# Fourth attention layer: row scores in eight one-bank pieces, and a ring of five banks for the turned score groups

## The chip, the cores and the metric

The kernel runs on one core of one Trainium2 chip. The metric is the device time of one execution in microseconds (us), the median of three runs. The profile is one further execution, recorded by the hardware profiler. Its own time is given beside the span of its trace.

## The reference, cut to what matters

Four transformer layers run one after the other on x (4 batches, 256 rows, 128 columns), each an attention over a context of 1601 rows and then a feed-forward block. The change is in the fourth attention, 16 heads of 8 columns:

```python
Q = _split(q @ Wq.T + bq)          # q: layer norm of x, (4, 256, 128)
K = _split(k @ Wk.T + bk)          # k, v: ctx_1024, (4, 1601, 128)
V = _split(v @ Wv.T + bv)
scores = jnp.einsum('bhqd,bhkd->bhqk', Q, K) / np.sqrt(HEAD_DIM)
scores = jnp.where(mask == 0, -1000000000.0, scores)
attn = jax.nn.softmax(scores, axis=-1)
out = jnp.einsum('bhqk,bhkd->bhqd', attn, V)
return merged(out) @ Wo.T + bo
```

There are 4 x 16 = 64 pairs of batch and head, called units here. Each has 256 x 1601 scores.

## The kernel before, in words

The stage is `quad_attention_stage` (L1221), called once, for this layer. It computes the scores of each unit twice. The first time they are **row scores**: queries on the partitions, keys along the row, only so that VectorE can find each query's largest score. The second time they are **turned scores**: keys on the partitions, queries along the row. The maxima are added to them through six more rows of the matmul's operands, so ScalarE can take the exponent directly, and the result already lies as the product with the values wants it.

The work of one step s of the loop, on each engine:

- TensorE, `score_piece(s, n)` (L1309 to L1321): row scores of unit s in four pieces (two halves of the 128-query tiles, and two halves of the keys, 801 and 800 wide). One piece fills 801 of the 1024 columns of a double bank, `S_WIDE[n % 2]`, by two matmuls (512 and 289 or 288 columns). The two double banks take turns. The piece waits until VectorE has drained the piece two before it (semaphore `drained`).
- VectorE, `maximum(s, n)` (L1480 to L1494): waits for the piece (`scored`), adds the mask and takes the maximum. In the trace it is a CUSTOM_DVE_ANT_0 and a short DVE_READ_ACCUMULATOR2_ANT behind it. After each second unit one TENSOR_REDUCE (L1494, called nmx below) joins the maxima.
- GpSimd cuts the maxima in three bf16 parts (L1467 to L1473), TensorE brings them into rows (`rows(s)`, L1346, in even steps), and ScalarE copies them to the operands `qx` (L1447).
- TensorE, `turned_group(s, g)` (L1323 to L1337): turned scores of unit s - 3 (`TURN = 3`) in seven groups W0 to W6 of two key tiles each (W6 has one). A key tile is a mask matmul (L1335) and a score matmul (L1336), 256 columns each, added up in one bank. The groups, the rows and two rarer items take banks from the ring `BANKS` in turn, three banks before. A group waits until the item that had its bank three items earlier has been read (`bank_free`, L1296).
- ScalarE, `exponent(s, g)` (L1431): the exponent of one group, bank to SBUF.
- TensorE, `values(s)` (L1364): each four units make a quad. Its product with the values stands in two chunks at the front of two successive steps, 28 and 24 matmuls in fp32. So two steps of four have such a chunk. `turn_u` (L1375) turns the result once in each quad, and VectorE's `normalise` (L1504 to L1507) divides by the sum.

All engines run their own queue in program order. TensorE's order in a step, in which S0 to S3 are the four score pieces, is written out by hand:

```python
for s in range(LAST):
    values(s)
    turned_group(s, 0)
    score_piece(s, 0)
    turned_group(s, 1)
    turned_group(s, 2)
    score_piece(s, 1)
```

and then mix, W3, rows, turn_u, W4, S2, W5, output, S3, W6. VectorE does maxima 0, 1, 2, then `normalise`, then maximum 3. SyncE loads the operands of a unit once the turned scores of the unit six before it are through (`RING = 6`). PSUM has eight banks: three in the ring, one for the values' product, and the two double banks of the row scores.

Of the kernel before, what the change touches and what calls it, by code (L numbers as in the profile page):

```python
# [7 lines left out]
F32 = mybir.dt.float32  # L8
BF16 = mybir.dt.bfloat16
I32 = mybir.dt.int32  # L10
ALU = mybir.AluOpType
# [3 lines left out]
P = 128  # L15
D = 128
B, S, SC = 4, 256, 1601
# [5 lines left out]
LOWEST = -3.0e38  # L23
# [1197 lines left out]
def quad_attention_stage(core, name, acc, wot, load_operands, load_values, ks, qx, vs, mask, maskT):  # L1221
# [3 lines left out]
    UNITS, QUADS = B * HEADS, B * HEADS // 4  # L1225
    RING, PRT, V_RING = 6, 6, 3
    TURN = 3
    half = (SC + 1) // 2
    PIECES = [(qt, at, min(half, SC - at)) for qt in range(2) for at in (0, half)]
    GROUPS = [(kt, min(2, KT - kt)) for kt in range(0, KT, 2)]  # L1230
    NG = len(GROUPS)
    CHUNKS = [(0, 7), (7, KT)]
# [3 lines left out]
     recip_done, normed, mixed, mixed_out, out_ready, added, setup) = (core.sem(f"{name}_{s}") for s in names)  # L1236
    loaded = [core.sem(f"{name}_loaded{i}") for i in range(RING)]
    v_loaded = [core.sem(f"{name}_v_loaded{i}") for i in range(V_RING)]
    S_WIDE, BANKS, U_BANK = core.wide, core.bank[0:3], core.bank[3]
    LAST = UNITS + TURN + 4  # L1240

    with ExitStack() as ctx:
        junk = core.sb(ctx, name + "_junk", [P, 2, half], F32)
        prT = core.sb(ctx, name + "_prT", [P, PRT, KT, S], F32)
        mx = core.sb(ctx, name + "_mx", [P, 2, 2, 2, 2], F32)
        nmx = core.sb(ctx, name + "_nmx", [P, 2, 2, 2], F32)
        rest = core.sb(ctx, name + "_rest", [P, 2, 2], F32)
        zero = core.sb(ctx, name + "_zero", [P, 2, 2], F32)
# [27 lines left out]
        at_slot = {slot: n for n, slot in enumerate(slots)}  # L1276

        def bank_of(s, item):
            return BANKS[at_slot[s, item] % 3]

        @block.sync
        def _(sp):
# [11 lines left out]
        @block.tensor  # L1294
        def _(pe):
            def bank_free(s, item):  # L1296
                if at_slot[s, item] < 3:
                    return
                t, before = slots[at_slot[s, item] - 3]
                if before == "rows":  # L1300
                    pe.wait_ge(rows_in, pair_rows(t) + 1)
                elif before == "mix":
                    pe.wait_ge(mixed_out, batch_end(t) + 1)
                elif before == "out":
                    pe.wait_ge(added, batch_end(t) + 1)
                else:
                    pe.wait_ge(exp_done, NG * (t - TURN) + int(before[1:]) + 1)

            def score_piece(s, n):  # L1309
                if not s < UNITS:  # L1310
                    return
                if n == 0:
                    pe.wait_ge(loaded[s % RING], 32 * (s // RING + 1))
                if 4 * s + n >= 2:
                    pe.wait_ge(drained, 4 * s + n - 1)
                qt, at, w = PIECES[n]
                for c in range(0, w, 512):
                    m = min(512, w - c)
                    ins = pe.matmul(S_WIDE[n % 2][:, c:c + m], qx[0:72, s % RING, qt * P:(qt + 1) * P],  # L1319
                                    ks[0:72, s % RING, at + c:at + c + m], start=True, stop=True)  # L1320
                ins.then_inc(scored, 1)  # L1321

            def turned_group(s, g):  # L1323
# [45 lines left out]
            def turn_u(s):  # L1369
                if quad_chunk(s) is None or quad_chunk(s)[1] != len(CHUNKS) - 1:  # L1370
                    return
                q = quad_chunk(s)[0]
                pe.wait_ge(u_out, q + 1)
                for qt in range(2):
                    ins = pe.transpose(U_BANK[:, S + qt * P:S + (qt + 1) * P], u_sb[:, qt * P:(qt + 1) * P], core.ident[:, :])  # L1375
                ins.then_inc(u_turned, 1)
# [20 lines left out]
                ins.then_inc(out_ready, 1)  # L1397

            for s in range(LAST):
                values(s)  # L1400
                turned_group(s, 0)
                score_piece(s, 0)
                turned_group(s, 1)
                turned_group(s, 2)
                score_piece(s, 1)
                mix(s)
                turned_group(s, 3)
                rows(s)
                turn_u(s)
                turned_group(s, 4)  # L1410
                score_piece(s, 2)
                turned_group(s, 5)
                output(s)
                score_piece(s, 3)
                turned_group(s, 6)

        @block.scalar
        def _(act):
# [56 lines left out]
        @block.vector  # L1475
        def _(dve):
            dve.memset(prT[:, :, KT - 1, :], 0.0).then_inc(setup, 1)
            dve.memset(U_BANK[:, 0:S], 0.0).then_inc(setup, 1)

            def maximum(s, n):  # L1480
                if not s < UNITS:
                    return
                p, e = s // 2, s % 2
                qt, at, w = PIECES[n]
                dve.wait_ge(scored, 4 * s + n + 1)
                if e == 0 and n == 0 and p >= 2:
                    dve.wait_ge(max_ready, p - 1)
                dve.tensor_tensor_reduce(junk[:, n % 2, 0:w], S_WIDE[n % 2][:, 0:w], mask(qt, at, w), 1.0, LOWEST, ALU.add, ALU.max,  # L1488
                                         mx[:, p % 2, qt, e, n % 2:n % 2 + 1]).then_inc(drained, 1)
                if e == 1 and n == 3:  # L1490
                    dve.wait_ge(drained, 4 * s + 4)
                    if p >= 2:
                        dve.wait_ge(cut_done, p - 1)
                    dve.tensor_reduce(nmx[:, p % 2, :, :], mx[:, p % 2, :, :, :], X, ALU.max, negate=True).then_inc(max_ready, 1)  # L1494

            def normalise(s):
                if quad_chunk(s) is None or quad_chunk(s)[1] != len(CHUNKS) - 1:
                    return
                q = quad_chunk(s)[0]
                lanes = U_BANK[:, S:2 * S].rearrange("p (t j c) -> p t j c", t=2, j=4)  # L1500
                dve.wait_ge(u_turned, q + 1)
                if q % 4 == 0 and q > 0:
                    dve.wait_ge(mixed, q // 4)
                dve.reciprocal(rtot[:, :, :], lanes[:, :, :, 8]).then_inc(recip_done, 1)  # L1504
                dve.wait_ge(recip_done, q + 1)
                out = heads_out[:, :, q % 4 * 32:(q % 4 + 1) * 32].rearrange("p t (j d) -> p t j d", j=4)
                dve.tensor_tensor(out, lanes[:, :, :, 0:8], rtot[:, :, :].unsqueeze(3).broadcast_to([P, 2, 4, 8]),  # L1507
                                  ALU.mult).then_inc(normed, 1)

            for s in range(LAST):  # L1510
                maximum(s, 0)
                maximum(s, 1)
                maximum(s, 2)
                normalise(s)
                maximum(s, 3)
                if batch_end(s) is not None:
                    b = batch_end(s)
                    tiles = acc[:, 2 * b:2 * b + 2, :]
                    dve.wait_ge(out_ready, b + 1)
                    dve.tensor_tensor(tiles, tiles, bank_of(s, "out")[:, 0:S].rearrange("p (t d) -> p t d", t=2),  # L1520
                                      ALU.add).then_inc(added, 1)
            dve.wait_ge(added, B)
# [602 lines left out]
def pair_layer(core, name, acc, wq, wk, wv, wo):  # L2125
# [29 lines left out]

    PIECES = [(0, 1024), (1024, SC - 1024)]

# [398 lines left out]
```

## Time and profile before

| | before |
|---|---|
| median of 3 runs | 2402.89 us (2401.49 to 2403.2) |
| profiled execution, its own time | 2405.89 us |
| span of its trace | 2404.1 us |
| mean granted TensorE clock | 0.911 |
| TensorE busy, whole span | 2066.4 us (86%) |
| VectorE busy, whole span | 1358.7 us (57%) |
| ScalarE busy, whole span | 1327.5 us (55%) |
| the stage that is changed | first row score at 1960.7 us, last at 2339.0 us |

A matmul's record is longer than the time for which it holds the engine, since matmuls overlap. What TensorE spends on one is read as the distance from its start to the start of the next. A granted clock of 1.00 is the 2.4 GHz level; a lower mean in a window is a mixture with the 1.2 GHz level. PEld is TensorE's load of the weights for the next matmul; "issue" as the releaser means that the profile shows nothing that was waited for.

### The profile page before, as it was taken

What the parts mean: (1) busy time and instruction counts of PE and PEld (TensorE: products, weight loads), DVE (VectorE), ACT (ScalarE), POOL (GpSimd) and SP (SyncE); (2) the same over time, 40 slices, a digit from 0 to 9 for tenths busy, and PEclk for the clock granted to TensorE, in tenths of its full rate; (3) what the DMA queues carried; (4) which work ended last, traced back from release to release, by engine and by line L of the source; (5) the groups of instructions that cost most, each with busy time, mean ns of one, the idle gap of its engine ahead of it and who ended that gap; (6) DMA issues with size and microseconds to landing.
All of it is one profiled execution on the core that took longest, in us unless ns stands there. A gap on an engine that the chain in (4) does not pass through costs nothing. (4 is left out here: it accounts for less than half of the span.)

```text
span 2404.1 us, 44599 instructions
## 1 busy us (share of the span) xinstructions
PE 2066.4 (86%) x17629; PEld 1438.3 (60%) x17629; DVE 1358.7 (57%) x3398; ACT 1327.5 (55%) x2088; POOL 100.6 (4%) x335
## 2 busy tenths in 40 slices
PE   5499999945844799799999999999994559999997
PEld 3377777723632467577777777777772326666663
DVE  4588888865442521555555545545545556666662
ACT  3499999931312733355555555555552326676763
POOL 1000000000011200000000000000000310000000
PEclk9699999976875989899999999999996669999997
DMA  6411111103232011000000000000000631111110
GB/s 216 168 58 53 53 56 54 46 14 114 80 102 89 4 36 35 36 1 1 1 1 1 1 1 1 2 1 1 1 1 10 228 117 60 52 59 54 58 37 13
DMA packets 50709, 115.32 MB, mean 48 GB/s; under 512 B 6476, under 2 KB 26732, under 8 KB 50508
## 3 DMA queue, kind: packets, MB, share of 16 engines
q1 hardware_dynamic: 44172, 82.25, 11.0%
q0 software_dynamic: 6336, 30.28, 3.6%
q8 instruction: 139, 2.28, 0.4%
q14 instruction: 62, 0.51, 0.1%
HBM read 81.71 MB, written 30.80 MB: 47 GB/s over the span
## 5 line engine op out<-in xcount | busy, mean ns | idle before, releaser
L2316 ACT ACTIVATE a_prT<-bank 128x512 f32<-128x512 f32 (+1 forms) x448 | 232.7, 565 | 328.0 <-PE bank L2225 327.8
L1488 DVE CUSTOM_DVE_ANT_0 a_attn_junk<-wide,a_mask 128x801 f32<-128x801 f32 (+1 forms) x256 | 247.0, 992 | 125.5 <-PE wide L1319 124.1
L1431 ACT ACTIVATE a_attn_prT<-bank 128x512 f32<-128x512 f32 (+1 forms) x448 | 237.2, 566 | 119.7 <-PE bank L1336 98.3
L2341 DVE CUSTOM_DVE_ANT_0 a_sc<-wide,a_zeros 128x1024 f32<-128x1024 f32 (+1 forms) x256 | 243.1, 988 | 91.8 <-PE wide L2211 91.8
L1777 DVE CUSTOM_DVE_ANT_0 a_attn_sc<-wide,a_mask 128x801 f32<-128x801 f32 (+1 forms) x256 | 252.9, 989 | 18.4 <-PE wide L1631 16.2
L1647 PE MATMUL bank<-ident,a_attn_sc 128*128 128x128 f32 x1664 | 244.9, 276 | 15.3 <-ACT a_attn_prT L1736 14.1
L1647 PEld LDWEIGHTS bank<-ident,a_attn_sc 128*128 128x128 f32 x1664 | 198.8, 141 | 62.6 <-issue 42.7
L2225 PE MATMUL bank<-ident,a_sc 128*128 128x128 f32 x1664 | 231.2, 277 | 1.5 <-ACT a_prT L2316 1.5
L2225 PEld LDWEIGHTS bank<-ident,a_sc 128*128 128x128 f32 x1664 | 185.4, 141 | 54.4 <-issue 28.1
L1742 ACT ACTIVATE a_attn_sc<-a_attn_sc,a_attn_nmx 128x1601 f32<-128x1601 f32 x128 | 209.6, 1638 | 8.5 <-DVE a_attn_nmx L1783 8.5
L2211 PE MATMUL wide<-a_kT,a_qT 64*128 64x512 f32 (+1 forms) x1024 | 211.0, 529 | 0.0
L2277 PEld LDWEIGHTS bank<-a_prT,a_vt 128*64 128x64 f32 x3328 | 180.3, 137 | 48.4 <-issue 47.0
L2325 ACT ACTIVATE a_sc<-a_sc,a_nmx 128x1601 f32<-128x1601 f32 x128 | 207.1, 1623 | 3.4 <-DVE a_nmx L2368 3.4
L1335 PE MATMUL bank<-a_maskT,identb 128*128 128x256 bf16 (+1 forms) x832 | 201.2, 275 | 2.2 <-DVE x L1520 1.9
L1336 PE MATMUL bank<-a_qx,a_ks 128*128 128x256 bf16 (+1 forms) x832 | 199.9, 273 | 0.0
L2277 PE MATMUL bank<-a_prT,a_vt 128*64 128x128 f32 x3328 | 195.8, 275 | 0.9 <-ACT a_prT L2316 0.9
L1736 ACT ACTIVATE a_attn_prT<-bank 128x512 f32<-128x512 f32 x320 | 172.6, 582 | 31.5 <-PE bank L1647 28.7
L1631 PE MATMUL wide<-a_ks,a_qx 72*128 72x512 bf16 (+2 forms) x512 | 152.6, 340 | 9.3 <-DMA a_qx<-a_q_stack 8.4
L2211 PEld LDWEIGHTS wide<-a_kT,a_qT 64*128 64x128 f32 x1024 | 88.6, 186 | 102.4 <-issue 93.2
L1319 PE MATMUL wide<-a_ks,a_qx 72*128 72x512 bf16 (+2 forms) x512 | 134.2, 345 | 9.6 <-DMA a_qx<-a_q_stack 8.3
L2242 PE MATMUL bank<-a_wv,ctxT 128*128 128x128 f32 x832 | 119.4, 282 | 1.3 <-ACT a_vt L2316 0.7
L2236 PE MATMUL bank<-ctxT,a_wk 128*128 128x512 f32 (+1 forms) x256 | 117.3, 543 | 2.7 <-ACT a_kT L2316 1.4
(432 smaller groups left out, 2800.7 us busy)
## 6 DMA issues: line engine op xcount, KB each, us to landing
a_ks<-a_k_parts SPq DMA_DIRECT2D x128, 225.1 KB
a_proj_ctxb<-in_ctxT SPq DMA_DIRECT2D x12, 832.0 KB, 5.1
a_k_parts<-a_proj_kp POOLq DMA_DIRECT2D x24, 416.0 KB, 5.7
a_v_rows<-a_proj_vb POOLq DMA_DIRECT2D x8, 936.0 KB, 8.4
a_vs<-a_v_rows SPq DMA_DIRECT2D x32, 234.0 KB
a_q_stack<-a_proj_qp POOLq DMA_DIRECT2D x18, 256.0 KB, 4.4
a_qx<-a_q_stack SPq DMA_DIRECT2D x128, 36.0 KB
ctxT<-in_ctxT SPq DMA_DIRECT2D x4, 832.0 KB, 12.7
```

Source lines behind the costliest of these rows:

```text
L1335: pe.matmul(out, core.identb[:, 0:keys], maskT(kt + j), start=True, stop=False)
L1431: act.activation(prT[0:keys, u % PRT, kt:kt + m, :], bank_of(s, f"W{g}")[0:keys, 0:m * S].rearrange("p (t q) -> p t q", q=S), ACT.Exp).the ...
L1488: dve.tensor_tensor_reduce(junk[:, n % 2, 0:w], S_WIDE[n % 2][:, 0:w], mask(qt, at, w), 1.0, LOWEST, ALU.add, ALU.max, mx[:, p % 2, qt, e, ...
L1647: ins = pe.transpose(bank_of(s, f"T{g}")[:, j * P:(j + 1) * P], sc[:, u % 2, qt, kt * P:(kt + 1) * P], core.ident[:, :])
L1742: act.activation(sc[:, s % 2, qt, 0:SC], sc[:, s % 2, qt, 0:SC], ACT.Exp, bias=nmx[:, s % 2, qt:qt + 1], scale=1.0).then_inc(exp_done, 1)
L1777: dve.tensor_tensor_reduce(sc[:, s % 2, qt, at:at + w], S_WIDE[n % 2][:, 0:w], mask(qt, at, w), 1.0, LOWEST, ALU.add, ALU.max, mx[:, s % 2 ...
L2211: ins = pe.matmul(S_WIDE[h][:, c:c + w], qT[rows, slot, qt * P:(qt + 1) * P], kT[rows, slot, at + c:at + c + w], start=True, stop=True)
L2225: ins = pe.transpose(RING[k % 3][:, (j % 4) * P:(j % 4 + 1) * P], flat(t)[:, j * P:(j + 1) * P], core.ident[:, :])
L2277: ins = pe.matmul(U_BANK[DH * h:DH * (h + 1), 0:P], vt[:, slot, kt, DH * h:DH * (h + 1)], prT[:, KT * h + kt, :], start=(kt == 0), stop=(k ...
L2316: copy = lambda out, src: act.activation(out, src, ACT.Copy)
L2325: act.activation(sc[:, s % 2, h, 0:SC], sc[:, s % 2, h, 0:SC], ACT.Exp, bias=nmx[:, s % 2, h:h + 1], scale=1.0, accum_out=tot[:, s % 4, h: ...
L2341: dve.tensor_tensor_reduce(sc[:, s % 2, h, at:at + w], S_WIDE[h][:, 0:w], zeros[:, 0:w], 1.0, LOWEST, ALU.add, ALU.max, mx[:, s % 2, h, p: ...
```

## The change

The row scores of a unit come in eight pieces (four of up to 401 keys for each of the two query tiles, 401, 401, 401 and 398), one matmul and one bank each. Two banks, 4 and 5 (together the former `wide0`), take turns. Banks 6 and 7 (the former `wide1`) join the ring, which has five banks then. TensorE's order is written anew, and VectorE takes eight maxima for a unit.

```diff
--- before.py
+++ after.py
@@ -1225,8 +1225,10 @@
     UNITS, QUADS = B * HEADS, B * HEADS // 4
     RING, PRT, V_RING = 6, 6, 3
     TURN = 3
-    half = (SC + 1) // 2
-    PIECES = [(qt, at, min(half, SC - at)) for qt in range(2) for at in (0, half)]
+    PARTS = 4
+    width = (SC + PARTS - 1) // PARTS
+    PIECES = [(qt, at, min(width, SC - at)) for qt in range(2) for at in range(0, SC, width)]
+    NP = len(PIECES)
     GROUPS = [(kt, min(2, KT - kt)) for kt in range(0, KT, 2)]
     NG = len(GROUPS)
     CHUNKS = [(0, 7), (7, KT)]
@@ -1236,13 +1238,14 @@
      recip_done, normed, mixed, mixed_out, out_ready, added, setup) = (core.sem(f"{name}_{s}") for s in names)
     loaded = [core.sem(f"{name}_loaded{i}") for i in range(RING)]
     v_loaded = [core.sem(f"{name}_v_loaded{i}") for i in range(V_RING)]
-    S_WIDE, BANKS, U_BANK = core.wide, core.bank[0:3], core.bank[3]
+    S_BANK, BANKS, U_BANK = core.bank[4:6], core.bank[0:3] + core.bank[6:8], core.bank[3]
+    NB = len(BANKS)
     LAST = UNITS + TURN + 4
 
     with ExitStack() as ctx:
-        junk = core.sb(ctx, name + "_junk", [P, 2, half], F32)
+        junk = core.sb(ctx, name + "_junk", [P, 2, width], F32)
         prT = core.sb(ctx, name + "_prT", [P, PRT, KT, S], F32)
-        mx = core.sb(ctx, name + "_mx", [P, 2, 2, 2, 2], F32)
+        mx = core.sb(ctx, name + "_mx", [P, 2, 2, 2, PARTS], F32)
         nmx = core.sb(ctx, name + "_nmx", [P, 2, 2, 2], F32)
         rest = core.sb(ctx, name + "_rest", [P, 2, 2], F32)
         zero = core.sb(ctx, name + "_zero", [P, 2, 2], F32)
@@ -1276,7 +1279,7 @@
         at_slot = {slot: n for n, slot in enumerate(slots)}
 
         def bank_of(s, item):
-            return BANKS[at_slot[s, item] % 3]
+            return BANKS[at_slot[s, item] % NB]
 
         @block.sync
         def _(sp):
@@ -1294,9 +1297,9 @@
         @block.tensor
         def _(pe):
             def bank_free(s, item):
-                if at_slot[s, item] < 3:
+                if at_slot[s, item] < NB:
                     return
-                t, before = slots[at_slot[s, item] - 3]
+                t, before = slots[at_slot[s, item] - NB]
                 if before == "rows":
                     pe.wait_ge(rows_in, pair_rows(t) + 1)
                 elif before == "mix":
@@ -1311,13 +1314,11 @@
                     return
                 if n == 0:
                     pe.wait_ge(loaded[s % RING], 32 * (s // RING + 1))
-                if 4 * s + n >= 2:
-                    pe.wait_ge(drained, 4 * s + n - 1)
+                if NP * s + n >= 2:
+                    pe.wait_ge(drained, NP * s + n - 1)
                 qt, at, w = PIECES[n]
-                for c in range(0, w, 512):
-                    m = min(512, w - c)
-                    ins = pe.matmul(S_WIDE[n % 2][:, c:c + m], qx[0:72, s % RING, qt * P:(qt + 1) * P],
-                                    ks[0:72, s % RING, at + c:at + c + m], start=True, stop=True)
+                ins = pe.matmul(S_BANK[n % 2][:, 0:w], qx[0:72, s % RING, qt * P:(qt + 1) * P],
+                                ks[0:72, s % RING, at:at + w], start=True, stop=True)
                 ins.then_inc(scored, 1)
 
             def turned_group(s, g):
@@ -1397,22 +1398,26 @@
                 ins.then_inc(out_ready, 1)
 
             for s in range(LAST):
+                score_piece(s, 0)
                 values(s)
                 turned_group(s, 0)
-                score_piece(s, 0)
+                score_piece(s, 1)
                 turned_group(s, 1)
+                score_piece(s, 2)
                 turned_group(s, 2)
-                score_piece(s, 1)
+                score_piece(s, 3)
                 mix(s)
                 turned_group(s, 3)
                 rows(s)
                 turn_u(s)
+                score_piece(s, 4)
                 turned_group(s, 4)
-                score_piece(s, 2)
+                score_piece(s, 5)
                 turned_group(s, 5)
                 output(s)
-                score_piece(s, 3)
+                score_piece(s, 6)
                 turned_group(s, 6)
+                score_piece(s, 7)
 
         @block.scalar
         def _(act):
@@ -1482,13 +1487,13 @@
                     return
                 p, e = s // 2, s % 2
                 qt, at, w = PIECES[n]
-                dve.wait_ge(scored, 4 * s + n + 1)
+                dve.wait_ge(scored, NP * s + n + 1)
                 if e == 0 and n == 0 and p >= 2:
                     dve.wait_ge(max_ready, p - 1)
-                dve.tensor_tensor_reduce(junk[:, n % 2, 0:w], S_WIDE[n % 2][:, 0:w], mask(qt, at, w), 1.0, LOWEST, ALU.add, ALU.max,
-                                         mx[:, p % 2, qt, e, n % 2:n % 2 + 1]).then_inc(drained, 1)
-                if e == 1 and n == 3:
-                    dve.wait_ge(drained, 4 * s + 4)
+                dve.tensor_tensor_reduce(junk[:, n % 2, 0:w], S_BANK[n % 2][:, 0:w], mask(qt, at, w), 1.0, LOWEST,
+                                         ALU.add, ALU.max, mx[:, p % 2, qt, e, n % PARTS:n % PARTS + 1]).then_inc(drained, 1)
+                if e == 1 and n == NP - 1:
+                    dve.wait_ge(drained, NP * (s + 1))
                     if p >= 2:
                         dve.wait_ge(cut_done, p - 1)
                     dve.tensor_reduce(nmx[:, p % 2, :, :], mx[:, p % 2, :, :, :], X, ALU.max, negate=True).then_inc(max_ready, 1)
@@ -1508,11 +1513,11 @@
                                   ALU.mult).then_inc(normed, 1)
 
             for s in range(LAST):
-                maximum(s, 0)
-                maximum(s, 1)
-                maximum(s, 2)
+                for n in range(6):
+                    maximum(s, n)
                 normalise(s)
-                maximum(s, 3)
+                maximum(s, 6)
+                maximum(s, 7)
                 if batch_end(s) is not None:
                     b = batch_end(s)
                     tiles = acc[:, 2 * b:2 * b + 2, :]
```

What stands in the queues of before and of the changed kernel is shown at two places.

TensorE before, from the last groups of one step to the next (L1319 is a score piece, L1335 and L1336 a turned group, L1364 the values):

```order
L1336 MATMUL bank1<-a3_qx,a3_ks 128x256
L1319 MATMUL wide1<-a3_ks,a3_qx 128x512
L1319 MATMUL wide1<-a3_ks,a3_qx 128x288
L1335 MATMUL bank2<-a3_maskT,identb 65x256
L1336 MATMUL bank2<-a3_qx,a3_ks 65x256
L1364 MATMUL bank3<-a3_attn_prT,a3_vs 9x256 x24
L1335 MATMUL bank0<-a3_maskT,identb 128x256
L1336 MATMUL bank0<-a3_qx,a3_ks 128x256
L1335 MATMUL bank0<-a3_maskT,identb 128x256
L1336 MATMUL bank0<-a3_qx,a3_ks 128x256
L1319 MATMUL wide0<-a3_ks,a3_qx 128x512
L1319 MATMUL wide0<-a3_ks,a3_qx 128x289
```

The same place on TensorE in the changed kernel (its L1320 is a score piece, L1336 and L1337 a turned group, L1365 the values):

```order
L1337 MATMUL bank0<-a3_qx,a3_ks 128x256
L1320 MATMUL wide0<-a3_ks,a3_qx 128x401
L1336 MATMUL bank1<-a3_maskT,identb 65x256
L1337 MATMUL bank1<-a3_qx,a3_ks 65x256
L1320 MATMUL wide0<-a3_ks,a3_qx 128x398
L1320 MATMUL wide0<-a3_ks,a3_qx 128x401
L1365 MATMUL bank3<-a3_attn_prT,a3_vs 9x256 x24
L1336 MATMUL bank2<-a3_maskT,identb 128x256
L1337 MATMUL bank2<-a3_qx,a3_ks 128x256
```

The last group of a step has one key tile. Before, it and the whole W0 of the next step (and the values, where there are some) stood between S3 and S0. Now S6, the short W6, S7 and the next unit's S0 follow one another, with nothing between S7 and S0, and the values come behind S0.

VectorE before, around the join of the maxima (ISA with two operands is the maximum, ISA without one reads it out):

```order
L1488 ISA a3_attn_mx 128x1
L1488 ISA a3_attn_junk,a3_attn_mx<-wide1,a3_mask 128x800
L1488 ISA a3_attn_mx 128x1
L1488 ISA a3_attn_junk,a3_attn_mx<-wide0,a3_mask 128x801
L1488 ISA a3_attn_mx 128x1
```

VectorE in the changed kernel:

```order
L1493 ISA a3_attn_junk,a3_attn_mx<-wide0,a3_mask 128x401
L1493 ISA a3_attn_mx 128x1
L1493 ISA a3_attn_junk,a3_attn_mx<-wide0,a3_mask 128x398
L1493 ISA a3_attn_mx 128x1
L1499 TENSOR_REDUCE a3_attn_nmx<-a3_attn_mx 128x4
L1493 ISA a3_attn_junk,a3_attn_mx<-wide0,a3_mask 128x401
```

Each maximum covers half the columns, and there are twice as many, all out of the two banks of the former `wide0`.

## Rows read from the trace of the kernel before

**Rows 1.** The page: span, and granted clock in 40 slices
```profile
span 2404.1 us, 44599 instructions
PEclk9699999976875989899999999999996669999997
```
**Rows 2.** Windows: length; PE, PEld, DVE, ACT, POOL busy; PEclk; DMA share; GB/s
```profile
400.00:500.00 100.00, 96.04 (x1015) 70.04 (x1017) 80.08 (x188) 88.22 (x115) 0.00 (x0) 1.00 0.12 38
600.00:640.00 40.00, 32.20 (x141) 20.71 (x141) 19.23 (x69) 13.26 (x19) 0.53 (x1) 0.79 0.34 131
...
2070.00:2110.00 40.00, 39.33 (x395) 26.93 (x394) 27.07 (x61) 27.15 (x53) 2.47 (x12) 1.00 0.16 47
```
**Rows 3.** Waits, 1950 to 2360 us: who <- whom: us in total, times, longest
```profile
DVE a_attn_junk L1488 <- PE wide L1319: 124.1, 119, 5.0
ACT a_attn_prT L1431 <- PE bank L1336: 98.3, 38, 3.3
...
PEld bank L1335 <- issue: 14.2, 34, 0.5
...
PEld bank L1346 <- POOL a_attn_parts L1473: 4.0, 14, 1.3
...
PEld bank L1335 <- ACT a_attn_prT L1431: 2.1, 11, 0.3
...
PE wide L1319 <- DVE a_attn_mx L1488: 1.2, 4, 0.4
```
**Rows 4.** Timeline of PE, a step's end: start us, us, engine, line
```profile
2119.69 0.51 PE L1319 MATMUL wide<-a_ks,a_qx 72*128 72x512 bf16 x2
2120.04 0.27 PE L1335 MATMUL bank<-a_maskT,identb 128*128 128x256 bf16 x1
...
2120.47 0.51 PE L1319 MATMUL wide<-a_ks,a_qx 72*128 72x512 bf16 x2
2120.82 0.27 PE L1335 MATMUL bank<-a_maskT,identb 128*65 128x256 bf16 x1
...
2121.13 2.56 PE L1364 MATMUL bank<-a_attn_prT,a_vs 128*9 128x256 f32 x44
```
**Rows 5.** Timeline of DVE in the same stretch
```profile
2120.24 1.00 DVE L1488 CUSTOM_DVE_ANT_0 a_attn_junk<-wide,a_mask 128x801 f32<-128x801 f32 x1 [0.22 <-PE wide L1319]
...
2121.15 0.99 DVE L1488 CUSTOM_DVE_ANT_0 a_attn_junk<-wide,a_mask 128x800 f32<-128x800 f32 x1
2122.07 0.08 DVE L1488 DVE_READ_ACCUMULATOR2_ANT a_attn_mx<- 128x1 f32 x1
2122.18 0.16 DVE L1494 TENSOR_REDUCE a_attn_nmx<-a_attn_mx 128x4 f32<-128x8 f32 x1
```
**Rows 6.** Timeline of DVE in the third layer: the same operation, 577 wide
```profile
1509.08 0.75 DVE L2341 CUSTOM_DVE_ANT_0 a_sc<-wide,a_zeros 128x577 f32<-128x577 f32 x1
...
1509.75 0.76 DVE L2341 CUSTOM_DVE_ANT_0 a_sc<-wide,a_zeros 128x577 f32<-128x577 f32 x1
```
**Rows 7.** Timeline of the stage's first steps, at a clock below full
```profile
1962.48 0.08 DVE L1488 DVE_READ_ACCUMULATOR2_ANT a_attn_mx<- 128x1 f32 x1
...
1962.62 0.13 PEld L1319 LDWEIGHTS wide<-a_ks,a_qx 72*128 72x128 bf16 x2 [1.15 <-DVE a_attn_mx L1488]
...
1966.58 0.13 PEld L1319 LDWEIGHTS wide<-a_ks,a_qx 72*128 72x128 bf16 x2 [0.97 <-DVE a_attn_mx L1488]
```
**Rows 8.** Timeline, full clock: POOL lets the rows' matmuls go
```profile
2159.14 0.21 POOL L1473 TENSOR_TENSOR a_attn_parts<-a_attn_rest,a_attn_parts 128x4 bf16<-128x4 f32 x1
...
2159.43 0.09 PEld L1346 LDWEIGHTS bank<-identb,a_attn_parts 128*6 128x6 bf16 x2 [0.21 <-POOL a_attn_parts L1473]
...
2159.63 0.28 PE L1335 MATMUL bank<-a_maskT,identb 128*128 128x256 bf16 x1
```
**Rows 9.** Timeline of DVE: normalise in two successive quads
```profile
2128.85 0.20 DVE L1504 RECIPROCAL a_attn_rtot<-bank 128x8 f32<-128x8 f32 x1
...
2129.23 0.98 DVE L1488 CUSTOM_DVE_ANT_0 a_attn_junk<-wide,a_mask 128x800 f32<-128x800 f32 x1
...
2152.78 0.20 DVE L1504 RECIPROCAL a_attn_rtot<-bank 128x8 f32<-128x8 f32 x1
```

## The prediction, on record before the changed kernel ran

> **What bounds the kernel now.** I read the windows first, then the waits, then the timeline. The changed stage runs at the end of the program, and the slices of the page show the clock near full there [rows 1]. In a window of the stage TensorE is busy for 39.33 of 40 us at a granted clock of 1.00, the 2.4 GHz level, while VectorE and ScalarE are busy for 27 us each [rows 2]. The waits say the same: VectorE waits 124.1 us for score pieces and ScalarE 98.3 us for turned groups, while TensorE's matmuls waited 1.2 us for VectorE, in 4 cases at the stage's start; a weight load waited 2.1 us for ScalarE, in 11 cases [rows 3]. So TensorE's queue is the path. Every 0.1 us that it stands still in each of the 64 steps costs 6.4 us, and VectorE has only to keep out of its way.
>
> The timeline gives TensorE's prices. A piece of 801 columns holds it from 2119.69 to 2120.04, 0.35 us. From there to the next piece are one whole group, 0.43 us. The short W6 stands from 2120.82 to about 2121.03 (two matmuls at 0.108), 0.22 us, and then the values start [rows 4]. A quad takes 2152.78 - 2128.85 = 23.93 us [rows 9].
>
> **What the change takes and adds on TensorE.** The columns stay the same (1601 for each query tile), and so does the number of score matmuls, 8 per unit: 512 + 289 becomes 401 + 401. By the row, 401 columns take 0.35 x 401/801 = 0.17 us [rows 4]. Groups, values and loads are the same. The streaming term is 0. The operands of S0 are wanted earlier by the length of the values, at most 3 us; SyncE orders them steps ahead, at the end of the turned group of the unit six before, so I put it at nothing.
>
> **The ring of five banks.** It can only remove waits for a bank. They are the 2.1 us above [rows 3], 0.1% of the time. ScalarE's 98.3 us of waiting is not cured by banks, since TensorE produces groups no faster. I take -2 us, with 0 as the other end.
>
> **The two banks of the row scores: the round.** A bank is used in a round: matmul, VectorE's maximum, release, next matmul. Its parts:
> - From the start of a piece to the start of its maximum: 2119.69 to 2120.24 is 0.55 us for 801 columns [rows 4, 5]. 0.34 of it is streaming, so the latency is 0.21 and for 401 columns it makes 0.17 + 0.21 = 0.38 us.
> - From a maximum to the next thing that VectorE can start: 0.91 us at 801 columns [rows 5] and 0.67 at 577 [rows 6]. That is 0.00107 us a column, so 401 columns take 0.67 - 176 x 0.00107 = 0.48 us. If none of it shrank below the 577 row it would be 0.67, the upper bound. I take 0.49.
> - From there (the start of the read-out) to TensorE's weight load: 1962.48 to 1962.62, 0.14 us [rows 7]. A load that has waited isn't hidden behind a running matmul. At the rows' matmuls GpSimd ends at 2159.35, the load starts at 2159.43, and the next group starts at 2159.63; the two small matmuls stream for 0.11 us, so streaming began near 2159.52, 0.09 after the load began [rows 8]. That gives 0.24 us together, 0.14 at least.
>
> The round is 0.38 + 0.49 + 0.24 = 1.11 us, and 1.01 with the lower end. So piece n + 2 can't start earlier than 1.11 us behind piece n.
>
> **Where TensorE gives that much time and where not.** With a whole group between pieces it comes to the piece after next 2 x (0.17 + 0.43) = 1.20 us later. That is more than 1.11, so there is no wait. At the end of a step it is different: S6 0.17, W6 0.22, S7 0.17, and then S0 of the next unit at once, 0.56 us behind S6. S0 needs the bank of S6. The wait is 1.11 - 0.56 = 0.55 us (0.45 with the lower end), in every step, also where the values follow, since they stand behind S0. S7 itself waits 0.13 us for the bank of S5, which is inside the same sum. Before, the pieces were 1.2, 1.2 and more, 0.78 and 1.2 us apart and the same comparison never failed. All of W0, the values and the groups are queued behind S0, and ScalarE waits for them.
>
> I work it out for the 60 boundaries that have turned groups and a next unit (steps 3 to 62): 60 x 0.55 = 33.0 us. Once in a quad `normalise` stands between maxima 5 and 6. It delays the next maximum by the 0.38 us from the reciprocal to the next maximum [rows 9]. VectorE was free 0.11 us before S6's maximum was due, so S0 is late by another 0.27 us: 14 x 0.27 = 3.8 us. The join nmx starts 0.11 us after a read-out begins and delays the maximum of S0 [rows 5]; that adds about 0.05 us for S2 in one step of four, 0.7 us in all.
>
> **The start.** In steps 0 to 2 there are no groups. Before, such a step took 1966.58 - 1962.62 = 3.96 us [rows 7]. At half the clock a round is 0.33 + 0.21 + 0.49 + 0.24 = 1.27 us, eight pieces 5.1 us, so 3 x 1.1 = +3.3 us.
>
> **Given back.** The rows' matmuls waited 4.0 us for GpSimd in 14 cases [rows 3]. The maxima of a pair are complete at about the same place as before, and `rows` stands later behind it by the new wait, so some of this goes: -1 us.
>
> **Sum.** +33.0 + 3.8 + 0.7 + 3.3 - 2 - 1 = +37.8 us on the profiled execution's 2405.89, which lies 3.0 us above the median of the runs. Against the median: 2402.89 + 38 = 2441 us, 1.6% slower. The lower ends (0.45 a boundary, nothing for the start, 5 us given back) leave 27.0 + 4.5 - 5 = +26, so 2429.
>
> **A rule that speaks against it.** In the window of the stage the clock was granted in full with TensorE busy for 98% [rows 2]. With the new waits a quad takes 23.93 + 2.5 = 26.4 us and TensorE is busy for 90% of it. The nearest rows on both sides are 96% busy at 1.00 and 80% busy at 0.79 [rows 2]. The Trainium skill, page "TensorE: Matmul & The Clock Gate", section "A second HAM failure mode: psum-queue depth-cycling", says that short pauses between groups of matmuls that cycle through PSUM banks can make the clock swing between its two levels. No row here shows that for pauses of half a microsecond, so it is only a rival.
>
> **The rivals.**
> 1. *The round is longer than 1.20 us.* Then a wait arises at every second piece as well. If the maximum of 401 columns cost 0.67 us, as at 577, the round would be 1.29 us: 0.73 us at each boundary and 0.09 at each of three more pairs, 1.0 us a step, so 60 + 4 + 6 = +70 us, 2473. For it: a cost that doesn't halve with the width is unseen below 577. Against it: the two widths give a straight line through nearly nothing but columns. Chance 0.13.
> 2. *The clock falls.* If TensorE ran at 1.2 GHz for a tenth of the stage's 380 us, that tenth would do half its work, another 38 us: 2479. Against it: pauses are short and the stage stays 90% busy. Chance 0.06.
> 3. *No change.* The wait at S0 is made good elsewhere, because TensorE wasn't the path after all. Then its busy 39.33 of 40 us would have to hide idle time, such as the 14.2 us at 34 loads put down to issue [rows 3]. Time within 5 us of 2403. Chance 0.05.
> 4. *Faster.* The five banks count for more: if these 14.2 us before the groups are waits for a bank, and the round hides behind a ring in which groups run ahead, the sum is -14.2 - 2.1 = -16 us, 2387. It decides if the load waits at L1335 vanish and S0 shows none. Against it: the loads wait where the piece ahead still streams, and the matmuls behind show no gap. And the round at S0 is a sum of durations that I read, of which 0.38 + 0.49 alone exceeds the 0.56 available. Chance 0.04.
>
> **How the numbers follow.** My forecast (waits at the step boundary only, 2425 to 2450) has a chance of 0.72. A measurement of this kernel tells about 0.2%, 5 us, from no change. Slower: 0.72 + 0.13 + 0.06 = 0.91, same 0.05, faster 0.04. The predicted time is that of the forecast, 2441. The range has to leave out no more than 2 in 10: below it reaches 2420, since the faster cases hold 0.09, and above 2468, which takes in most of rival 1.
>
> **What the profile after would show.** If I am right: L1320 waits for the maximum (L1493) once in each step, about 0.5 us, at S0; VectorE's maximum lasts about 0.57 us with a pitch of 0.49; the quad takes 26 to 27 us; the clock stays at 1.00; no wait of L1336 for ScalarE. A wait at pieces with a whole group between them means rival 1. A clock under 1.00 in the middle of the stage means rival 2. A quad of 24 us or less means that my reading of the path is wrong.

## The result, and the profile after

| | before | changed |
|---|---|---|
| median on the same chip | 2402.45 us (4 runs, 2401.49 to 2403.2) | 2437.77 us (4 runs, 2436.13 to 2440.51) |
| ratio, 95% interval | | 1.0148 [1.0131, 1.0166] |
| span of the profiled execution | 2404.1 us | 2434.4 us |

The change made the kernel 35 us slower; 38 us were forecast. First, from the page of the changed kernel, the granted clock in 40 slices, VectorE's maximum and the score matmul:

```profile
PEclk9799999966966899999999999999995679999997
...
L1493 DVE CUSTOM_DVE_ANT_0 a_attn_junk<-wide,a_mask 128x401 f32<-128x401 f32 (+1 forms) x512 | 287.2, 574 | 122.5 <-PE wide L1320 113.9
...
L1320 PE MATMUL wide<-a_ks,a_qx 72*128 72x401 bf16 (+1 forms) x512 | 176.6, 346 | 36.2 <-DVE a_attn_mx L1493 27.7
```

The score matmuls (now L1320) have idle time ahead of them, and it ends with VectorE's maximum. The waits of the stage show the same pair, 27.7 us in 71 cases, where it was 1.2 us in 4 [rows 3]:

```profile
ACT a_attn_prT L1436 <- PE bank L1337: 94.8, 42, 4.0
ACT a_attn_prT L1436 <- PE wide L1337: 54.9, 27, 4.0
PEld wide L1320 <- issue: 40.6, 63, 0.8
...
PE wide L1320 <- DVE a_attn_mx L1493: 27.7, 71, 0.6
...
PEld bank L1336 <- issue: 8.2, 19, 0.4
...
PEld wide L1336 <- issue: 4.7, 11, 0.4
...
PEld bank L1347 <- POOL a_attn_parts L1478: 0.3, 1, 0.3
```

The 63 loads put down to issue (40.6 us) are those of the 63 pieces S0 behind the first: the load stands behind the same wait as its matmul, and the profile names no releaser for it. No line has a wait of the turned groups for ScalarE any more, and ScalarE waits longer than before, 150 us. The timeline of TensorE shows the end of a step without values. It answers to [rows 4]:

```profile
2119.79 0.34 PE L1320 MATMUL wide<-a_ks,a_qx 72*128 72x401 bf16 x1
...
2120.40 0.34 PE L1320 MATMUL wide<-a_ks,a_qx 72*128 72x401 bf16 x1
2120.58 0.27 PE L1336 MATMUL wide<-a_maskT,identb 128*65 128x256 bf16 x1
2120.69 0.27 PE L1337 MATMUL wide<-a_qx,a_ks 128*65 128x256 bf16 x1
2120.80 0.34 PE L1320 MATMUL wide<-a_ks,a_qx 72*128 72x398 bf16 x1
2121.50 0.33 PE L1320 MATMUL wide<-a_ks,a_qx 72*128 72x401 bf16 x1 [0.36 <-DVE a_attn_mx L1493]
```

```profile
2121.47 0.10 PEld L1320 LDWEIGHTS wide<-a_ks,a_qx 72*128 72x128 bf16 x1 [0.58 <-issue]
```

S5 starts at 2119.79, S6 at 2120.40, S7 at 2120.80 and S0 at 2121.50, that is 1.10 us behind S6. S7 streams for 0.17 us, so TensorE stands for 0.53 us. The 0.36 in the record is less, because the record of S7 runs on after its columns are in. VectorE at the same moment, to be read with [rows 5]:

```profile
2120.66 0.08 DVE L1493 DVE_READ_ACCUMULATOR2_ANT a_attn_mx<- 128x1 f32 x1
2120.77 0.58 DVE L1493 CUSTOM_DVE_ANT_0 a_attn_junk<-wide,a_mask 128x401 f32<-128x401 f32 x1
2121.27 0.08 DVE L1493 DVE_READ_ACCUMULATOR2_ANT a_attn_mx<- 128x1 f32 x1
2121.27 0.57 DVE L1493 CUSTOM_DVE_ANT_0 a_attn_junk<-wide,a_mask 128x398 f32<-128x398 f32 x1
```

S6 starts, 0.37 us later its maximum, 0.50 us later the read-out, 0.23 us later S0. That is the whole round of the bank that S0 takes. The steady steps repeat it: S0 stands for 0.53 us in 46 of the 60 boundaries that the prediction counted and for 0.79 us in the other 14, those with `normalise` ahead, 35.4 us in all. In the step with `normalise` it is longer, and a quad, read from one reciprocal to the next, has gone from 23.93 us [rows 9] to 26.47 us (of `normalise`, the reciprocal is its first instruction):

```profile
2115.64 0.20 DVE L1509 RECIPROCAL a_attn_rtot<-bank 128x8 f32<-128x8 f32 x1
...
2142.11 0.20 DVE L1509 RECIPROCAL a_attn_rtot<-bank 128x8 f32<-128x8 f32 x1
```

```profile
2141.84 0.34 PE L1320 MATMUL wide<-a_ks,a_qx 72*128 72x401 bf16 x1
...
2142.25 0.34 PE L1320 MATMUL wide<-a_ks,a_qx 72*128 72x398 bf16 x1
2143.21 0.33 PE L1320 MATMUL wide<-a_ks,a_qx 72*128 72x401 bf16 x1 [0.62 <-DVE a_attn_mx L1493]
```

Here S0 comes 1.37 us behind S6 and TensorE stands for 0.79 us. The window that answers to [rows 2] shows TensorE busy for 37.39 of 40 us, with the clock still at 1.00:

```profile
2070.00:2110.00 40.00, 37.39 (x394) 23.69 (x396) 26.93 (x98) 23.34 (x45) 2.47 (x12) 1.00 0.18 53
```

The start of the stage answers to [rows 7]:

```profile
1956.46 0.85 PE L1320 MATMUL wide<-a_ks,a_qx 72*128 72x401 bf16 x2 [8.27 <-DMA a_qx<-a_q_stack]
...
1961.33 0.92 PE L1320 MATMUL wide<-a_ks,a_qx 72*128 72x401 bf16 x2 [0.28 <-DVE a_attn_mx L1493]
...
2387.15 5.80 PE L1365 MATMUL bank<-a_attn_prT,a_vs 128*9 128x256 f32 x104 [0.47 <-ACT a_attn_prT L1436]
```

Eight pieces take 4.87 us there, where four took 3.96, both at the clock's lower level (0.50). From the first score piece (1956.46) to the start of the last product with the values (2387.15) the stage takes 430.7 us. Before, the same two points lay 392.4 us apart (1960.68 and 2353.09), so the stage is 38.3 us longer. The spans differ by 30.3 us only: in this pair of profiles the code ahead of the stage took 4.2 us less and the code behind it 3.8 us less, though neither was touched. Single executions of one kernel lie that far apart (29 runs of the kernel before on one chip: 2393 to 2405 us).

### The profile page after: what moved, and what is told of

It is laid out like the page before. It is cut to its first block and busy times, and to the rows that moved or that the text cites. A ratio compares the mean times of both kernels' runs of the same rounds, so it can differ in the third digit from the quotient of the medians.

```text
span 2434.4 us, 45111 instructions
## 1 busy us (share of the span) xinstructions
PE 2071.1 (85%) x17629; PEld 1435.8 (59%) x17629; DVE 1400.7 (58%) x3910; ACT 1329.4 (55%) x2088; POOL 100.6 (4%) x335
## 5 line engine op out<-in xcount | busy, mean ns | idle before, releaser
L1493 DVE CUSTOM_DVE_ANT_0 a_attn_junk<-wide,a_mask 128x401 f32<-128x401 f32 (+1 forms) x512 | 287.2, 574 | 122.5 <-PE wide L1320 113.9
L1320 PE MATMUL wide<-a_ks,a_qx 72*128 72x401 bf16 (+1 forms) x512 | 176.6, 346 | 36.2 <-DVE a_attn_mx L1493 27.7
L1436 ACT ACTIVATE a_attn_prT<-bank 128x512 f32<-128x512 f32 (+1 forms) x271 | 146.8, 565 | 96.9 <-PE bank L1337 94.8
L1636 PE MATMUL wide<-a_ks,a_qx 72*128 72x512 bf16 (+2 forms) x512 | 152.4, 340 | 9.3 <-DMA a_qx<-a_q_stack 8.5
L1436 ACT ACTIVATE a_attn_prT<-wide 128x512 f32<-128x512 f32 (+1 forms) x177 | 97.1, 569 | 56.2 <-PE wide L1337 54.9
L1336 PE MATMUL bank<-a_maskT,identb 128*128 128x256 bf16 (+1 forms) x501 | 124.9, 274 | 0.0
L1337 PE MATMUL bank<-a_qx,a_ks 128*128 128x256 bf16 (+1 forms) x501 | 124.0, 273 | 0.0
```

What stands on the lines that cost most here:

```text
L1320: ins = pe.matmul(S_BANK[n % 2][:, 0:w], qx[0:72, s % RING, qt * P:(qt + 1) * P], ks[0:72, s % RING, at:at + w], start=True, stop=True)
L1436: act.activation(prT[0:keys, u % PRT, kt:kt + m, :], bank_of(s, f"W{g}")[0:keys, 0:m * S].rearrange("p (t q) -> p t q", q=S), ACT.Exp).the ...
L1493: dve.tensor_tensor_reduce(junk[:, n % 2, 0:w], S_BANK[n % 2][:, 0:w], mask(qt, at, w), 1.0, LOWEST, ALU.add, ALU.max, mx[:, p % 2, qt, e, ...
```

## The experiments

The theory: two banks are one too few. A bank comes round in 1.10 us, and at the end of a step TensorE wants it after 0.56. The rivals were: the number of pieces costs (semaphore waits, more instructions); the order costs (S0 ahead of the values); the ring of five gives something back and hides a larger loss. Each ratio below is against the kernel before on the same chip, with its 95% interval.

**Three banks for the row scores, four in the ring.** Pieces and order stay.

```diff
-    S_BANK, BANKS, U_BANK = core.bank[4:6], core.bank[0:3] + core.bank[6:8], core.bank[3]
+    S_BANK, BANKS, U_BANK = core.bank[4:7], core.bank[0:3] + core.bank[7:8], core.bank[3]
+    NS = len(S_BANK)
...
-                if NP * s + n >= 2:
-                    pe.wait_ge(drained, NP * s + n - 1)
+                if NP * s + n >= NS:
+                    pe.wait_ge(drained, NP * s + n - NS + 1)
```

(The bank and the scratch tile of a piece are then numbered by `(NP * s + n) % NS`.)

> Eight pieces and the changed order stay, the row scores get three banks (4, 5, 6) and the ring four. Theory of the round: a bank is wanted again by the third piece behind it. At the boundary of a step that is S5 to S0, 0.17 + 0.43 + 0.17 + 0.22 + 0.17 = 1.16 us, more than the round of 1.10, so the wait at S0 vanishes in every step, a quad takes about 23.9 us again, and in steps 0 to 2 VectorE's pitch of 0.50 us rules (eight pieces 4.0 us). Time 2402 us, between 2397 and 2407. Rival, the number of pieces costs (twice the semaphore waits and instructions on TensorE and VectorE): the time stays near 2437 us whatever the banks. Rival, the order costs (S0 ahead of the values): it stays near 2437 us too.

Measured: 2400.02 us against 2399.67, ratio 1.0 [0.999, 1.0011]. One bank more takes the loss away as far as the times can tell (0.1%, under 3 us), with eight pieces and with S0 ahead of the values. So neither of the rivals on pieces and order can be what cost 35 us. TensorE's timeline at the end of a step:

```profile
2106.57 0.34 PE L1321 MATMUL wide<-a_ks,a_qx 72*128 72x401 bf16 x1
2106.96 0.51 PE L1321 MATMUL wide<-a_ks,a_qx 72*128 72x398 bf16 x2
2107.40 3.21 PE L1366 MATMUL bank<-a_attn_prT,a_vs 128*9 128x256 f32 x56
```

S7 and S0 are one record of two now (x2), 0.51 us long: S0 starts at 2106.96 + 0.51 - 0.34 = 2107.13, right behind S7's 0.17 us of columns. The wait of 0.53 us is gone. A little is left all the same: a quad takes 24.18 us, where about 23.9 were expected, and the stage takes 394.0 us (1952.92 to 2346.91), 1.6 more than before. The runs with `turn_u` later, below, show where it lies.

```profile
2097.95 0.20 DVE L1510 RECIPROCAL a_attn_rtot<-bank 128x8 f32<-128x8 f32 x1
...
2122.13 0.20 DVE L1510 RECIPROCAL a_attn_rtot<-bank 128x8 f32<-128x8 f32 x1
```

**Four banks, a ring of three.** As above with `core.bank[4:8]` and `core.bank[0:3]`.

> As the run with three banks, but four banks for the row scores (4 to 7) and the ring of three as before the change. Theory of the round: no wait at S0; a ring of three costs what it cost before, 2 to 3 us in all; time 2403 us, between 2398 and 2408. Rival, a longer ring is worth something of its own: this run is slower than the one with four banks in the ring by 5 us or more.

Measured: 2399.63 us against 2399.67, ratio 1.0004 [0.9993, 1.0015]. On balance nothing changes: the stage takes 394.0 us again. The traces show two small effects that cancel. With the fourth bank a steady quad takes 24.07 us instead of 24.18; with the shorter ring each of the three quads over the end of a batch takes 25.43 us instead of 24.99.

**Two banks, a ring of three.** The changed kernel with banks 6 and 7 unused.

```diff
-    S_BANK, BANKS, U_BANK = core.bank[4:6], core.bank[0:3] + core.bank[6:8], core.bank[3]
+    S_BANK, BANKS, U_BANK = core.bank[4:6], core.bank[0:3], core.bank[3]
```

> The changed kernel with banks 6 and 7 left unused: two banks for the row scores, a ring of three. Theory: the ring of five is worth nothing to 2 us, since TensorE is the path and hardly waits for a bank; time 2438 us, between 2435 and 2443, quad 26.5 us. Rival, the five banks did give something back and hid a larger loss: this run is slower than the changed kernel by 5 to 16 us.

Measured: 2441.19 us against 2399.67, ratio 1.0174 [1.0158, 1.019]. The interval overlaps that of the changed kernel, [1.0131, 1.0166], which comes from another set of runs, so the times alone don't rule out the rival's smaller values (1.0174 against 1.0148 is 6 us). The profile decides. Its waits have the same line as the changed kernel's, and a quad is as long:

```profile
PE wide L1320 <- DVE a_attn_mx L1493: 27.7, 71, 0.6
...
PEld bank L1336 <- ACT a_attn_prT L1436: 1.8, 10, 0.3
```

```profile
2116.38 0.20 DVE L1509 RECIPROCAL a_attn_rtot<-bank 128x8 f32<-128x8 f32 x1
...
2142.84 0.20 DVE L1509 RECIPROCAL a_attn_rtot<-bank 128x8 f32<-128x8 f32 x1
```

26.46 us. From the first score (1958.02) to the last product (2388.65) the stage takes 430.6 us, against 430.7 with the ring of five. The two banks that the ring gained in the change are worth nothing there.

**Another order with two banks.** Ring of five as in the change.

```diff
-                score_piece(s, 0)
                 values(s)
                 turned_group(s, 0)
-                score_piece(s, 1)
+                score_piece(s, 0)
                 turned_group(s, 1)
-                score_piece(s, 2)
+                score_piece(s, 1)
                 turned_group(s, 2)
-                score_piece(s, 3)
+                score_piece(s, 2)
                 mix(s)
                 turned_group(s, 3)
+                score_piece(s, 3)
                 rows(s)
```

> Two banks and a ring of five as in the changed kernel, only TensorE's order is another: values, W0, S0, W1, S1, W2, S2, W3, S3, rows, turn_u, S4, then as changed. S7 and S0 have W0 between them, and the pair without a group between is S3, S4. Theory of the round (1.10 us): in steps without rows the wait moves to S4, 1.11 - 0.77 = 0.34 us, and S7 waits 0.12; in steps with rows 0.04 and 0.12; about 1.2 us a quad, and 0.3 for normalise, against 2.5 in the changed kernel. So about 15 us less than the changed kernel: 2421 us, between 2414 and 2428. Rival, the cost lies in the pieces and not in their places: 2437 us.

Measured: 2413.63 us against 2399.67, ratio 1.0058 [1.0039, 1.0077]. By the ratios that is 21 us less than the changed kernel, by place alone; 15 were expected, and the time lies just under the expected range. Why more, the timeline shows at a step with values and without rows:

```profile
2100.77 0.34 PE L1320 MATMUL wide<-a_ks,a_qx 72*128 72x401 bf16 x1
2101.38 0.75 PE L1320 MATMUL wide<-a_ks,a_qx 72*128 72x398 bf16 x2
```

```profile
2101.64 0.08 DVE L1493 DVE_READ_ACCUMULATOR2_ANT a_attn_mx<- 128x1 f32 x1
```

S3 and S4 are one record, so S4 starts at 2101.38 + 0.75 - 0.34 = 2101.79, only 1.02 us behind S2 and 0.15 us after the read-out of S2's maximum. The round was 1.11 in my sum and is 1.02 here. TensorE stands for 0.24 us (S3's columns were in at 2101.55), so S4 cost 0.24 us in such a step instead of 0.34, and S7 nothing instead of 0.12. S0 stands for 0.34 us once in a quad, in the step with `normalise`, and for 0.08 us in one step more:

```profile
2116.39 0.08 DVE L1493 DVE_READ_ACCUMULATOR2_ANT a_attn_mx<- 128x1 f32 x1
```

```profile
2116.43 0.27 PE L1337 MATMUL bank<-a_qx,a_ks 128*128 128x256 bf16 x1
2116.62 0.33 PE L1320 MATMUL wide<-a_ks,a_qx 72*128 72x401 bf16 x1
```

The group ahead of this S0 is in at 2116.43 + 0.11 = 2116.54, and S0 starts 0.23 us after the read-out of S6's maximum, not 0.15; the last section comes back to this. A quad takes 24.87 us, 0.9 more than before; 1.5 were expected.

**Half of the maximum.** The changed kernel; each maximum reads 200 of 401 columns and leaves out the rest. TensorE has the same work, pieces and waits.

```diff
-                dve.tensor_tensor_reduce(junk[:, n % 2, 0:w], S_BANK[n % 2][:, 0:w], mask(qt, at, w), 1.0, LOWEST,
+                h = w // 2
+                dve.tensor_tensor_reduce(junk[:, n % 2, 0:h], S_BANK[n % 2][:, 0:h], mask(qt, at, h), 1.0, LOWEST,
```

> The changed kernel, but each of VectorE's maxima reads only the first half of its piece's columns (200 of 401; the other half is left out of the maximum). TensorE's work, its order, the number of pieces and all waits stay. Theory of the round: the maximum's pitch falls from 0.50 to about 0.29 us, the round from 1.10 to 0.89, the wait at S0 from 0.53 to 0.32 us in every step and from 0.79 to about 0.37 in the step with normalise, 1.1 us a quad, and the start gets 2 us shorter. Time about 18 us less than the changed kernel, that is 17 us above before (between 12 and 23). Rival, twice as many pieces and semaphore waits cost as such: no difference to the changed kernel, 35 us above before.

Measured: 2419.43 us against 2401.69, ratio 1.0079 [1.0057, 1.0102], 18 us above before (17 expected). TensorE's wait for the maximum, and one place of it:

```profile
PE wide L1320 <- DVE a_attn_mx L1494: 11.4, 63, 0.2
```

```profile
2113.97 0.08 DVE L1494 DVE_READ_ACCUMULATOR2_ANT a_attn_mx<- 128x1 f32 x1
```

```profile
2113.70 0.33 PE L1320 MATMUL wide<-a_ks,a_qx 72*128 72x398 bf16 x1
2114.21 0.33 PE L1320 MATMUL wide<-a_ks,a_qx 72*128 72x401 bf16 x1 [0.17 <-DVE a_attn_mx L1494]
```

S0 comes 0.34 us after S7's columns, where it was 0.53; the forecast was 0.32. VectorE was idle for about a third of the window before and after the change (27.07 and 26.93 of 40 us busy), and it sets TensorE's time through the length of a single instruction.

**Three banks, and turn_u later.**

```diff
                 rows(s)
-                turn_u(s)
                 score_piece(s, 4)
                 turned_group(s, 4)
+                turn_u(s)
```

> Three banks for the row scores and four in the ring, and turn_u behind W4 instead of behind the rows, so that ScalarE's copy of the values' product has 0.6 us more. In the run with three banks turn_u starts 0.43 us behind the rows' matmuls, which stream for 0.11. Theory: about 0.2 us a quad, 3 us in all, come back against that run: 1 to 4 us under before, so within what can hardly be told. Rival: the later normalise delays maxima 5 to 7 and S0 waits instead, no gain.

Measured: 2397.93 us against 2401.69, ratio 0.9986 [0.9974, 0.9998]. A quad takes 23.92 us, 0.26 less than with three banks alone, so what that run had left over lies at `turn_u`:

```profile
2097.20 0.20 DVE L1510 RECIPROCAL a_attn_rtot<-bank 128x8 f32<-128x8 f32 x1
...
2121.12 0.20 DVE L1510 RECIPROCAL a_attn_rtot<-bank 128x8 f32<-128x8 f32 x1
```

**Three banks, turn_u later, spread order.** The edits of the three-bank, the other-order and the last run together, with turn_u behind W4.

> As the run before, and TensorE's order is the spread one (values, W0, S0, W1, S1, W2, S2, W3, S3, rows, S4, W4, turn_u, S5, W5, S6, W6, S7). No bank is wanted sooner than 1.37 us. Theory: no wait for VectorE is left, also not in the step with normalise (0.1 us a quad in the run with three banks), a quad takes 23.7 to 23.8 us. 2 to 5 us under before. Rival: TensorE has no more to give and the time is that of before.

Measured: 2396.17 us against 2401.69, ratio 0.9987 [0.9973, 1.0]. A quad takes 23.80 us:

```profile
2097.33 0.20 DVE L1510 RECIPROCAL a_attn_rtot<-bank 128x8 f32<-128x8 f32 x1
...
2121.13 0.20 DVE L1510 RECIPROCAL a_attn_rtot<-bank 128x8 f32<-128x8 f32 x1
```

**The kernel before with turn_u later.** Four pieces in two double banks.

```diff
                 rows(s)
-                turn_u(s)
                 turned_group(s, 4)
+                turn_u(s)
```

> The kernel before with four pieces in two double banks, only turn_u stands behind W4. It tells whether what the last two runs may gain belongs to the pieces or to turn_u alone. Theory: 0.1 us a quad, 1 to 2 us under before, a quad takes 23.8 us. If the eight-piece runs gain 3 us or more and this one doesn't, smaller pieces are worth something of their own.

Measured: 2395.52 us against 2401.69, ratio 0.9988 [0.9976, 1.0]. A quad takes 23.79 us:

```profile
2097.44 0.20 DVE L1504 RECIPROCAL a_attn_rtot<-bank 128x8 f32<-128x8 f32 x1
...
2121.23 0.20 DVE L1504 RECIPROCAL a_attn_rtot<-bank 128x8 f32<-128x8 f32 x1
```

The last three have the same time, about 3 us under before by the ratios (their medians lie 4 to 6 us under), and moving turn_u alone is enough for it. In the profiles the stage takes 390.5 us in this last run and 388.4 in the one ahead of it, against 392.4 before. Eight pieces don't make a steady quad shorter: 23.80 us there and 23.79 here. The 2 us between the two stages lie mostly in the three quads over the end of a batch (24.73 against 25.25 us), and the medians don't show them. Only one of the three intervals lies clear of 1.0, so the gain is at the edge of what these runs can tell.

## Why the prediction was right, point by point

- **What bounds the stage.** Right: TensorE's queue is the path. Its standing time went into the result one for one.
- **Streaming term 0.** Right: with turn_u at the same place and enough banks, a quad takes 23.80 us with eight pieces and 23.79 with four. The term of nothing for S0's operands was right too: after the first piece of the stage no score matmul waits for a load from memory.
- **The round.** Right: 0.38 + 0.49 + 0.24 = 1.11 us were forecast, 0.37 + 0.50 + 0.23 = 1.10 measured. The maximum of 401 columns lasts 574 ns with a pitch of 0.50, as the two wider forms had it by a straight line. But the 0.24 of release fits S0 by luck. I had put it together from 0.14 us to the load, read at another piece [rows 7], and 0.09 from load to columns, read at the rows' matmuls [rows 8]. At S0 the load comes 0.20 us after the read-out (2121.27 to 2121.47) and the matmul 0.03 later. At S7 the whole release takes 0.14 us (2120.66 to 2120.80), my lower end. So my rule that no piece can start earlier than 1.11 us behind the piece two before it is wrong as it stands: S7 starts 1.01 us behind S5.
- **Where it bites.** Right: only at S0, once in each step, also ahead of the values. 0.55 forecast, 0.53 measured; with `normalise` 0.82 forecast, 0.79 measured. I had also charged 0.13 us to S7 inside the same sum; it hardly waited. One reading of the kernel before was wrong: from S3 to the next S0, without values, I had 1.2 us, but by my own prices it is 0.35 + 0.22 + 0.43 = 1.00, and the trace has 1.00 (2104.24 to 2105.24). From S2 to S0 that makes 1.78 us, against a round of 0.55 + 0.91 + 0.23 = 1.69 for 801 columns. No wait follows, as I said, but the kernel before had only 0.1 us to spare there.
- **The sum.** A quad was to grow by 2.5 us and grew by 26.47 - 23.93 = 2.54. The 60 boundaries were to cost 33.0 + 3.8 = 36.8 us and cost 35.4. The start was to cost 1.1 us a step and cost 4.87 - 3.96 = 0.91. The stage was to grow by 37.8 us and grew by 38.3; the medians moved by 35.3. The difference between the last two is no larger than the scatter of single executions. That the sum meets the stage within 0.5 us is luck in part, since its small misses have both signs. Boundaries and start came out about 2 us cheaper than forecast, and the 3 us given back did not come. Two things I had not seen, one at the ends of the batches and one at turn_u, nearly cancel: by estimate 3 x (1.96 - 2.54) = -1.7 and 16 x 0.12 = +1.9 us. The join of the maxima was to delay S2 in one step of four; S2 stood in three steps only, 0.2 us each, where VectorE also adds the output to x.
- **The ends of the batches: not seen.** The three quads over the end of a batch grew from 25.39 to 27.35 us, by 1.96 and not by 2.5. There the trace before has a wait for a bank that my list of such waits left out: a turned group waits until VectorE has added the output to x (L1520), because that output had the bank.

```profile
PE bank L1335 <- DVE x L1520: 1.9, 3, 0.6
```

With two score banks it is not the longer ring that takes this wait away: with the ring of three such a quad takes 27.35 us as well. It seems to have gone under the standing at S0; no run tests that by itself.

- **Given back: mis-sized.** I took -2 us for the ring and -1 for the rows. The ring gave nothing (the stage takes 430.7 us with five banks and 430.6 with three), so its term was too large, though its other end, 0, was in the range. The waits for GpSimd fell from 4.0 to 0.3 us as records, but the rows' matmuls were not earlier for it: in the steady steps they start, before and after, 0.20 us behind the matmul ahead of them. The other thing I didn't see is a small loss: turn_u starts 0.42 us behind the rows' matmuls (2139.93 and 2140.35), where it was 0.30, since, as I read it, less of TensorE's work now lies between W2 and turn_u while ScalarE copies (the rows stand below). Moving turn_u behind W4 took 0.26 us off a quad with three banks, and 0.14 off one of the kernel before. 3 x 0.53 + 0.79 + 0.12 = 2.50 us is nearly the whole growth of a quad.

The rows' matmuls and turn_u in the kernel before, and then in the changed one:

```profile
2150.31 0.28 PE L1346 MATMUL bank<-identb,a_attn_parts 128*6 128x128 bf16 x2
...
2150.61 0.44 PE L1375 MATMUL bank<-ident,a_attn_u 128*128 128x128 f32 x2
```

```profile
2139.93 0.28 PE L1347 MATMUL wide<-identb,a_attn_parts 128*6 128x128 bf16 x2
2140.35 0.44 PE L1376 MATMUL bank<-ident,a_attn_u 128*128 128x128 f32 x2
```

- **The rivals.** A round over 1.20 us: it was 1.10, and pieces with a whole group ahead of them did not wait, but for S2 at the three ends of batches. A falling clock: it stayed at 1.00, in this window and from 1976 to 2350 us, with 0.5 us of standing in each step. So the Trainium skill's case of a clock that swings with short pauses ("TensorE: Matmul & The Clock Gate", section "A second HAM failure mode: psum-queue depth-cycling") isn't this kernel's. The faster case needed the 14.2 us put down to issue to be waits for a bank: with the ring of five the same loads still wait 8.2 + 4.7 = 12.9 us for issue, and the stage is no shorter than with the ring of three.

## What to carry to other kernels

With a ring of buffers between two engines, compare the whole round (fill, latency, drain, release) with the time in which the filling engine comes back to the same buffer, at the tightest place of its order and not on average. Halving the pieces here left the latency and the release as they were and took the drain only from 0.91 to 0.50 us, so it takes more buffers, or the pieces must be spaced evenly: spacing alone gave back 21 of the 35 us. Buffers given to a ring that is hardly waited for buy next to nothing: here one bank moved from the ring of five to the row scores was worth 35 us.

## What the runs showed of the hardware that I had not expected

The release of a bank reaches TensorE in two sizes, and what sorts them is the piece and not how long TensorE has stood. S0 starts 0.23 us after the read-out of the maximum began, whether TensorE had stood for 0.53 us (2121.27 to 2121.50, the changed kernel), for 0.34 us (2113.97 to 2114.21, half of the maximum; rounding makes it 0.24) or for 0.08 us (2116.39 to 2116.62, the run with another order). For other pieces that had to wait it was 0.14 or 0.15 us: S4 of the run with another order, where TensorE had stood for 0.24 us (2101.64 to 2101.79), and S7 of the changed kernel (2120.66 to 2120.80).

In the program S0 is the only piece ahead of which TensorE waits for two semaphores, `loaded` and `drained`; the others wait for `drained` alone. The record of the execution has a semaphore instruction on TensorE, 0.05 us long, right ahead of S0's load, and none ahead of S4's in the run with another order. That this second wait makes the difference of 0.08 us fits all these places, but no run moved it, so it is not shown. Where the release takes 0.15 us, the 0.24 of my sum was too long, and that made the forecast for the other order too slow.
